# Two gather products of a four-layer graph network: finished chunk by chunk beside the products

## The reference

```python
h = jnp.maximum(_layernorm(x), 0.0)
# layer 3: GCN convolution with self loops, then mish
norm = dinv[row] * dinv[col]                 # dinv = rsqrt(degree + 1)
out = segment_sum((h @ W)[row] * norm[:, None], col) + b
x = x + mish(out)
h = jnp.maximum(_layernorm(x), 0.0)
# layer 4: mean over the neighbours
agg = segment_sum(h[src], dst) / maximum(deg, 1.0)[:, None]
x = x + relu(h @ W_self.T + b_self + agg @ W_neigh.T + b_neigh)
```

## Time and profile before

| | us |
|---|---|
| median of three runs | 3570.17 |
| lowest and highest | 3569.80, 3575.74 |
| the profiled execution | 3569.01 |
| its span | 3566.90 |
| PE busy | 2545.4 (71%) |
| DVE busy | 2710.3 (76%) |
| ACT busy, POOL busy | 1606.4 (45%), 1998.4 (56%) |

### The profile page before, as it was taken

How to read it: one execution, slowest core, us unless ns; L and a number is a source line. 1 busy time by engine, 2 the same in 40 slices (tenths; PEclk the granted TensorE clock), 3 DMA queues, 4 the chain that set the end, 5 groups by cost and what they waited for, 6 DMA issues and landing times. The chain is left out here.

```text
span 3566.9 us, 88132 instructions
## 1 busy us (share of the span) xinstructions
PE 2545.4 (71%) x20080; PEld 1940.4 (54%) x20081; DVE 2710.3 (76%) x8289; ACT 1606.4 (45%) x4084; POOL 1998.4 (56%) x2354
## 2 busy tenths in 40 slices
PE   2433555555555539999999999999992377779399
PEld 1222344343343428888888888888872122334245
DVE  8754777777777739999999999999977799810601
ACT  2011222222222227878787878787866433210201
POOL 1006777777777768888888888888860000000100
PEclk9976767777677669999999999999995699979697
DMA  9992222222222228888888888888866688566182
GB/s 382 414 413 75 81 77 81 77 77 82 77 77 82 72 76 225 228 228 228 224 229 228 229 224 227 230 229 226 227 223 267 249 297 299 212 242 219 75 331 72
DMA packets 699413, 696.66 MB, mean 195 GB/s; under 512 B 48174, under 2 KB 630528, under 8 KB 689632
## 3 DMA queue, kind: packets, MB, share of 16 engines
q1 hardware_dynamic: 478018, 536.77, 44.4%
q10 hardware_dynamic: 195550, 104.71, 12.1%
q0 software_dynamic: 25792, 54.52, 4.5%
HBM read 340.91 MB, written 354.90 MB: 195 GB/s over the span
## 5 line engine op out<-in xcount | busy, mean ns | idle before, releaser
L909 POOL DMA_INDIRECT sorted_rows<-rows,posi x806 | 782.2, 970 | 339.0 <-issue 317.1
L1191 DVE SCALAR_TENSOR_TENSOR acc<-acc,keep,pm 128x256 f32<-128x256 f32 x1504 | 718.3, 478 | 28.5 <-issue 13.1
L1018 POOL TENSOR_SCALAR ohs_e<-iota,rt 128x128 f32<-128x128 f32 x1128 | 661.4, 600 | 12.6 <-DMA rt<-sorted_rows 12.6
L1118 PE MATMUL pm<-ohw_e,ohs_e 128*128 128x128 f32 x3008 | 663.0, 302 | 0.0
L857 PE MATMUL s_peq<-sb_w1bb,eT 128*128 128x256 f32 x806 | 353.1, 532 | 394.9 <-ACT eT L712 376.0
L1027 POOL TENSOR_TENSOR hid<-pre_e,excess 128x512 f32<-128x512 f32 x376 | 517.3, 1376 | 144.5 <-ACT excess L1054 144.5
L1124 PE MATMUL px<-PN,dT 128*128 x4512 | 499.1, 220 | 0.2 <-ACT dT L1061 0.2
L1070 ACT ACTIVATE ohw_e<-ohd_e,rt 128x128 f32<-128x128 bf16 x1504 | 474.7, 386 | 0.0
L1118 PEld LDWEIGHTS pm<-ohw_e,ohs_e 128*128 128x128 f32 x3008 | 459.6, 193 | 0.0
L1135 PE MATMUL ps<-hid,ohs_e 128*128 128x129 f32 x3008 | 417.9, 281 | 1.5 <-POOL hid L1027 1.5
L857 PEld LDWEIGHTS s_peq<-sb_w1bb,eT 128*128 128x128 f32 x806 | 173.1, 265 | 437.2 <-ACT eT L712 428.9
(11 more groups left out here) (300 smaller groups left out, 4438.1 us busy)
## 6 DMA issues: line engine op xcount, KB each, us to landing
count_matrices<-acc SPq DMA_DIRECT2D x1504, 128.0 KB, 2.5
ab<-count_matrices SPq DMA_DIRECT2D x75, 1600.0 KB, 8.7
sorted_rows<-zrow SPq DMA_DIRECT2D x188, 528.0 KB, 10.4
rt<-sorted_rows ACTq DMA_DIRECT2D x184, 528.0 KB, 4.5
arb<-count_matrices SPq DMA_DIRECT2D x25, 1664.0 KB, 6.7
arb<-count_matrices SPq DMA_DIRECT2D x25, 1536.0 KB, 6.4
ef<-in_edge_attr_dram SPq DMA_DIRECT2D x58, 364.0 KB
sorted_rows<-rows,posi POOLq DMA_INDIRECT x806
```

Source lines behind the costliest of these rows:

```text
L909: pool.indirect_dma_start(sortd, bass.IndirectOffsetOnAxis(ap=posi[:, h, c:c + 1], axis=0), rows[:, h, c, :], None).then_inc(s_sc[h], 16)
L1018: last = nc.gpsimd.tensor_scalar(ohs[:, k % BUFS, j, :], iota128[:], rt[:, k, j, D + 1:D + 2], None, ALU.is_equal)
L1118: last = nc.tensor.matmul(pm[:, q, j % 2, P:2 * P], ohs[:, kp % BUFS, j, :], ohw[:, kp % BUFS, j, :], start=True, stop=True)
L1191: nc.vector.scalar_tensor_tensor(acc[:, k % SUMS, j, :], before, keep[:, at:at + 1] if isinstance(at, int) else keep[:, ds(at, 1)], pm[:, ...
```

## The change

Both gathers now run over seven chunks of destinations (six of 512, one of 128) instead of over source tiles. For each chunk PE adds the products of all 25 source tiles into one of two PSUM banks, then goes on with the next chunk, and the sums of the chunk before are finished meanwhile. A load is now a piece: five source tiles by 512 destinations, 2048 consecutive bytes at a time (512 in the last chunk), five slots as before. The first five pieces are issued in `layernorm(1)`, those of the second gather during the first. The features are multiplied with the weight before the gather (`weigh`, 25 products), and all 25 stationary tiles are kept. The sums come out turned, so PE transposes them back (`turn_sums`). In the first gather the mish, the next layernorm and its transposes run per chunk in the same block; POOL has no part in it any more. In the second one the self products (`self_terms`) stand between the products, and the output leaves per chunk at the end. The degree block goes into an earlier stage.

Of the removed lines only the heads are shown; they stand in full above.

```diff
-def evacuate(tag, num, AGT):
...
+            nc.vector.tensor_scalar(dinv[:, 2, :], DEG[:], 1.0, None, ALU.add).then_inc(s_rd, 1)
...
-R = 5
...
-def gather_product(tag, turn, scale, AGT):
...
-    gather_product("2", 0, dinv[:, 0, :], AGT)
...
-    layernorm(2)
-    gather_product("3", 1, None, AGT)
...
+SG = 5
+SLOTS = 5
+NC = len(CUTS)
+NSG = NT // SG
+PIECE = [(c, g) for c in range(NC) for g in range(NSG)] * 2
+ab = gsb("gab", [P, SLOTS, SG, BANK])
+hw = gsb("ghw", [P, NT, D])
+self_ = gsb("g_own", [P, NT, D])
+AG = gsb("g_sums", [P, 2, BANK])
+def tiles(c):
+    return range(4 * c, min(4 * c + 4, NT))
+def load_piece(sp, m):
+    c, g = PIECE[m]
+    a, b = CUTS[c]
+    sp.dma_start(ab[:, m % SLOTS, :, 0:b - a],
+                 arv[0, g * SG:(g + 1) * SG, :, a // P:b // P, :].rearrange("s p q c -> p s (q c)")).then_inc(s_gld[m % SLOTS], 16)
+def gather_chunk(pe, num, turn, c, between):
+    a, b = CUTS[c]
+    n = turn * NC + c
+    if c >= 2:
+        pe.wait_ge(s_ga, n - 1)
+    for s in range(NT):
+        m = n * NSG + s // SG
+        if s % SG == 0:
+            pe.wait_ge(s_gld[m % SLOTS], 16 * (m // SLOTS + 1))
+        if c == 0 and s % 4 == 0:
+            pe.wait_ge(s_gw, turn * NC + s // 4 + 1)
+        last = nc.tensor.matmul(num[:, c % 2, 0:b - a], hw[:, s, :], ab[:, m % SLOTS, s % SG, 0:b - a],
+                                start=(s == 0), stop=(s == NT - 1))
+        if s % SG == SG - 1:
+            last.then_inc(s_gpc, 1)
+        if s in between:
+            between[s]()
+def turn_sums(pe, tn, turn, c):
+    n = turn * NC + c
+    pe.wait_ge(s_ga, n + 1)
+    if c >= 2:
+        pe.wait_ge(s_gy, n - 1)
+    for t in tiles(c):
+        o = t % 4 * P
+        last = nc.tensor.transpose(tn[:, c % 2, o:o + P], AG[:, c % 2, o:o + P], ident[:])
+    last.then_inc(s_gt, 1)
+def copy_sums(act, num, turn, c):
+    a, b = CUTS[c]
+    n = turn * NC + c
+    act.wait_ge(s_gpc, (n + 1) * NSG)
+    if c >= 2:
+        act.wait_ge(s_gt, n - 1)
+    nc.scalar.activation(AG[:, c % 2, 0:b - a], num[:, c % 2, 0:b - a], ACT.Copy).then_inc(s_ga, 1)
+def weigh(pe, zp, turn, c, w):
+    n = turn * NC + c
+    if c >= 2:
+        pe.wait_ge(s_gw, n - 1)
+    for t in tiles(c):
+        o = t % 4 * P
+        last = nc.tensor.matmul(zp[:, c % 2, o:o + P], HT[:, t * P:(t + 1) * P], wl[w][:], start=True, stop=True)
+    last.then_inc(s_gz, 1)
+def first_loads(sp):
+    for m in range(SLOTS):
+        load_piece(sp, m)
+layernorm(1, first_loads)
...
+        def nodes(c):
+            pe.wait_ge(s_nh, c + 1)
+            if c >= 2:
+                pe.wait_ge(s_nc, c - 1)
+            for t in tiles(c):
+                o = t % 4 * P
+                last = nc.tensor.transpose(hp[:, c % 2, o:o + P], H[:, t, :], ident[:])
+            last.then_inc(s_nt, 1)
+        for c in range(NC):
+            weigh(pe, zp, 0, c, "W2")
+        for c in range(NC):
+            between = {}
+            if c >= 1:
+                between[4] = lambda c=c: turn_sums(pe, tn, 0, c - 1)
+            if c >= 2:
+                between[14] = lambda c=c: nodes(c - 2)
+            gather_chunk(pe, num, 0, c, between)
+        turn_sums(pe, tn, 0, NC - 1)
+        nodes(NC - 2)
+        nodes(NC - 1)
...
+        for c in range(NC):
+            stationary(c)
+        for c in range(NC):
+            copy_sums(act, num, 0, c)
+            exp(c)
+            nodes(c)
...
+        def mish(c):
+            k = len(tiles(c))
+            w = k * P
+            t0 = 4 * c
+            z, q, v = Z[:, c % 2, 0:w], Q[:, c % 2, 0:w], V[:, c % 2, 0:w]
+            dve.wait_ge(s_gt, c + 1)
+            for t in tiles(c):
+                o = t % 4 * P
+                last = nc.vector.scalar_tensor_tensor(Z[:, c % 2, o:o + P], tn[:, c % 2, o:o + P], dinv[:, 0, t:t + 1],
+                                                      self_[:, t, :], ALU.mult, ALU.add)
+            last.then_inc(s_gy, 1)
+            dve.wait_ge(s_gy, c + 1)
+            nc.vector.tensor_scalar(q, z, 20.0, None, ALU.min).then_inc(s_zm, 1)
+            dve.wait_ge(s_e, c + 1)
+            link(nc.vector.scalar_tensor_tensor(q, q, 2.0, q, ALU.add, ALU.mult))
+            link(nc.vector.tensor_scalar(v, q, 2.0, None, ALU.add))
+            nc.vector.reciprocal(v, v)
+            link(nc.vector.tensor_tensor(z, z, q, ALU.mult))
+            link(nc.vector.tensor_tensor(z, z, v, ALU.mult))
+            xs = X[:, t0:t0 + k, :].rearrange("p t d -> p (t d)")
+            nc.vector.tensor_tensor(xs, xs, z, ALU.add).then_inc(s_gx, 1)
+            dve.wait_ge(s_gx, c + 1)
+            for u in tiles(c):
+                last = nc.vector.bn_stats(stats[:, u, :], X[:, u, :])
+            link(last)
+            for u in tiles(c):
+                last = nc.vector.bn_aggr(mv[:, u, :], stats[:, u, :])
+            last.then_inc(s_mv, 1)
+            dve.wait_ge(s_sq, c + 1)
+            link(nc.vector.reciprocal(rstd[:, t0:t0 + k], rstd[:, t0:t0 + k]))
+            nc.vector.scalar_tensor_tensor(nbias[:, t0:t0 + k], mv[:, t0:t0 + k, 0], -1.0, rstd[:, t0:t0 + k],
+                                           ALU.mult, ALU.mult).then_inc(s_nb, 1)
...
+        for c in range(NC):
+            mish(c)
+            if c >= 1:
+                nodes(c - 1)
+        nodes(NC - 1)
...
+        for m in range(NC * NSG + SLOTS, 2 * NC * NSG):
+            sp.wait_ge(s_gpc, m - SLOTS + 1)
+            load_piece(sp, m)
+        for c in range(NC):
+            sp.wait_ge(s_gx, NC + c + 1)
+            a, b = CUTS[c]
+            if c < NC - 1:
+                sp.dma_start(out[a:b, :].rearrange("(t p) d -> p t d", p=P), X[:, a // P:b // P, :]).then_inc(s_out, 16)
+            else:
+                sp.dma_start(out[a:N, :], X[0:NR, NT - 1, :]).then_inc(s_out, 16)
...
+        def self_terms(c):
+            if c >= 2:
+                pe.wait_ge(s_sc, c - 1)
+            for t in tiles(c):
+                o = t % 4 * P
+                nc.tensor.matmul(sf[:, c % 2, o:o + P], HT[:, t * P:(t + 1) * P], wl["WsT"][:], start=True, stop=False)
+                last = nc.tensor.matmul(sf[:, c % 2, o:o + P], ones[0:1, :], brow["bs"][:], start=False, stop=True)
+            last.then_inc(s_sf, 1)
+        for c in range(NC):
+            weigh(pe, zp, 1, c, "WnT")
+        for c in range(NC):
+            between = {}
+            if c >= 1:
+                between[4] = lambda c=c: turn_sums(pe, tn, 1, c - 1)
+            if c < NC - 1:
+                between[12] = lambda c=c: self_terms(c)
+            if c == NC - 2:
+                between[20] = lambda c=c: self_terms(NC - 1)
+            gather_chunk(pe, num, 1, c, between)
+        turn_sums(pe, tn, 1, NC - 1)
...
+        def value(c):
+            k = len(tiles(c))
+            dve.wait_ge(s_gt, NC + c + 1)
+            dve.wait_ge(s_sc, c + 1)
+            if c >= 2:
+                dve.wait_ge(s_gx, NC + c - 1)
+            for t in tiles(c):
+                o = t % 4 * P
+                last = nc.vector.scalar_tensor_tensor(Z[:, c % 2, o:o + P], tn[:, c % 2, o:o + P], rdeg[:, t:t + 1],
+                                                      self_[:, t, :], ALU.mult, ALU.add)
+            last.then_inc(s_gy, 1)
+            dve.wait_ge(s_gy, NC + c + 1)
+            xs = X[:, 4 * c:4 * c + k, :].rearrange("p t d -> p (t d)")
+            nc.vector.scalar_tensor_tensor(xs, Z[:, c % 2, 0:k * P], 0.0, xs, ALU.max, ALU.add).then_inc(s_gx, 1)
```

More of the change, by code:

```diff
@@ L104, in build @@
         DEG = tsb("DEG", [P, NT])
+        dinv = tsb("dinv", [P, 3, NT])
+        rdeg = tsb("rdeg", [P, NT])
+        bbc = tsb("bbc", [P, D])
         S = tsb("S", [P, NT + 1, D + 1])
@@ L110, in build @@
         brow = {}
-        for name in ("b1", "b2", "c2", "bs", "bn", "bb2"):
+        for name in ("b1", "bs", "bn"):
             brow[name] = tsb("row_" + name, [1, D])
@@ L130, in build, with layernorm @@
         NQ = -(-NT // 4)
-        def layernorm(r):
+        def layernorm(r, ahead=None):
             with ExitStack() as ctx:
@@ L136, in layernorm, with _ @@
                 block = ctx.enter_context(nc.Block())
+                if ahead:
+                    @block.sync
+                    def _(sp):
+                        ahead(sp)
                 @block.vector
@@ L173, in _ @@
                             last.then_inc(s_ln["turned"], 1)
-        def evacuate(tag, num, AGT):
-            with nc.Block() as block:
-                @block.vector
-                def _(dve):
-                    for c, (a, b) in enumerate(CUTS[0::2]):
-                        nc.vector.tensor_copy(AGT[:, a:b], num[:, 2 * c, 0:b - a])
-                @block.scalar
-                def _(act):
-                    for c, (a, b) in enumerate(CUTS[1::2]):
-                        nc.scalar.activation(AGT[:, a:b], num[:, 2 * c + 1, 0:b - a], ACT.Copy)
         with ExitStack() as srt:
@@ L297, in _ @@
                         act.dma_start(to if to.shape[0] == ED else to[:], fr).then_inc(s_ld, 16)
```

(35 more changed lines are left out.)

315 lines of the change are left out of this document (109 added, 206 removed).

## The result

The changed kernel takes 3480.02 us, the median of four runs (3478.00 to 3483.75), where the kernel before takes 3571.33 on the same chip (four runs, 3569.80 to 3575.74): ratio 0.9744, 95% interval 0.9727 to 0.976, 91 us less. Forecast were 3494, 76 less. The profiled execution took 3479.23, its span 3477.4; against the 3569.0 of before that is 89.8.

What follows compares the result with a forecast made beforehand. PE bounds the gathers; most of 98.6 us where it stands nearly still should be hidden. First gather 171.2 plus second 172.4 make 343.6 against 419.4 us, 75.8 less: 3494 us, range 3476 to 3526.

Steps and rivals of the forecast that it cites:

- weigh: Before each gather's chunks: 25 products with the weight at the low clock, 0.43 us each, 10.8 us.
- the cold start: Start of the long products in each gather, before the clock is high: 2.2 us on top of 129.0.
- the transposes: Groups of four inserted in both gathers: 0.78 us a group, 7.0 us in the first gather, 3.9 in the second.
- the end of the first gather: Chunk 6 and the unhidden chain behind mish(5), through normalization and the one-tile chain to the barrier: 22.2 us.
- the pairs: Second gather: 25 self products, each with a one-row product, 0.64 us a pair, 16.0 us; bounds 11.0 and 32.0.
- The main step: Behind layernorm(1): most of the 98.6 us with PE nearly still leaves the path; PE stays the bound; 75.8 us less.
- The lower case of the range: Transposes in both gathers at half the price, if the high clock halves it: 6 us less.
- I take half: Second gather: a pair's 1.28 us at the low clock taken as 0.64 at the high clock.
- Rival 1: Clock falls at inserted work: 4.8 us at each of six self-product groups, 29 us, 3523; chance 0.14.
- the forecast's 3550: Rival's further case: clock also falls at the first gather's nine transpose groups, 27 us more; chance 0.03 within 0.14.
- Do the loads keep up?: Both gathers: 2048-byte runs need 284 and 264 GB/s; 415 taken, no cost; at 228, 47 us more.
- Nothing there: Block of degrees moved to an earlier stage, beside a transfer already waited for: costs nothing in its new place.

Runs made afterwards that it cites:

- first_only: Changed kernel with the second gather and final block as in the kernel before, degrees computed ahead: 3505.2 us, ratio 0.9813 to the kernel before.
- after2: The changed kernel run once more, unaltered, as base of the last group of runs: 3485.18 us, ratio 0.9753 to the kernel before.
- act_order: Changed kernel with ACT copying chunk 6's first-gather sums ahead of chunk 5's root and normalization: 3771.29 us on the 3856.34 us chip, ratio 0.9776.
- up: Kernel before with only the changed kernel's edits ahead of the gathers: 3565.2 us against 3570.38, ratio 0.9981.
- spread: Changed kernel with a chunk's four pairs apart, behind products 7, 10, 13 and 16: 3762.57 us on the 3856.34 us chip, ratio 0.9753.
- bias_dve: Changed kernel without the 25 one-row products, DVE adding the last layer's bias: 3748.51 us on the 3856.34 us chip, ratio 0.9722.
- bias2: Changed kernel without the 25 one-row products, DVE adding the bias, run in the last group: 3463.84 us, ratio 0.9692 to the kernel before.

## Why the prediction was right, and where its terms were off

The mechanism held, and the time lies in the range (3476 to 3526), 4 us above its low end. That the sum of the tail came within 5.4 us is in part luck: weigh (4.5), the cold start (4.4), the transposes (4.8) and the end of the first gather (1.0) were 14.7 us too dear, the pairs (4.8) and the falls of the clock (5.1) 9.9 us too cheap.

- *The main step*, that most of what stood alone (98.6 us) goes beside the products and PE stays the bound, is shown: 60.3 us by the first gather alone, 21 to 23 by the second, tail 420.1 to 338.8 and 337.1. The forecast's shares were 59.3 and 16.5, with the wait of 6.7 us in front of the second gather in the first share; first_only still pays that wait. Drawn as in the forecast, the stretches of the changed kernel give 230.5 - 162.9 = 67.6 and 188.9 - 175.3 = 13.6.
- *First gather, weigh* (10.8) was too dear, twice: 9.0 and 8.1. I took the low clock for all of it, but the clock rises within it. The stretches from 3140, 3142 and 3144 us:

```profile
3140.00:3142.00 2.00, 2.00 (x12) 2.00 (x10) 0.00 (x0) 0.40 (x2) 0.00 (x0) 0.50 0.04 8
3142.00:3144.00 2.00, 2.00 (x14) 1.88 (x13) 1.14 (x4) 1.53 (x7) 0.00 (x0) 0.76 0.00 0
3144.00:3146.00 2.00, 1.66 (x13) 1.52 (x13) 1.50 (x6) 1.79 (x8) 0.00 (x0) 1.00 0.00 0
```

  In after2 it rises later, 6.0 us after weigh's first product instead of 3.5, and there the first long product starts 9.4 us after weigh's first and not 8.7.
- *The cold start* (2.2 in each gather) is paid in weigh, and the long products begin at 1.00. I had charged weigh the low clock to its end and the long products the start as well: 4.4 us too much.
- *Transposes*: 0.44 a group and not 0.78, as 0.196 each had been read at the low clock: 14 groups, 4.8 us. The lower case of the range.
- *Self products*: 0.83 a pair and not 0.64, 4.8 us more than forecast. The term was mis-sized by the step "I take half": the high clock doesn't halve the price of a pair in which a one-row product follows a full one.
- *Rival 1* came true in part and at a third of its price. The clock did fall at groups of self products, but at 9 of 24, and at 1.7 us each and not 4.8, since the fall comes behind the group and not in it (a group followed by slow products takes 3.22 us from start to start like any other), and the long products were back at the high clock within 4 us. That makes 5 us in the profiled execution, 3 in after2. At transposes it never fell: chunks 0 to 5 of the first gather have clock 1.00 with nine groups in them, so the forecast's 3550 is out. The Trainium skill (TensorE: Matmul & The Clock Gate, Part 4: PE-mode transpose) says that transposes don't count as PE work; this trace gives no sign of it for four of them between long products.
- *The end of the first gather* (22.2): 21.2. Mish(5) takes 10.9 as said. Behind it the path goes over ACT (normalization, copy, table load, exponential, see act_order) and then over DVE for the one tile. The forecast let the table loads run while ACT idles; this one, 1.28 us, has no idle time to hide in.
- *Do the loads keep up?* They do, 387 GB/s against 284. The value taken, 415 from packets of 3.7 KB, was somewhat high. What the Trainium skill says (DMA: Bandwidth & Descriptors, "Why small descriptors are slow"), 3 cycles over the bytes' own, would give by estimate 407 from these 415 (64/67 over 116/119); the run measured 387, so the rule gives a part of the fall.
- *Nothing there* for the degrees was right in their new place: from the first transpose of that stage to the first product of the next one there are 21.5 us before, 21.8 and 21.5 in the two profiles of the changed kernel. What their old block cost in front of the gather no run shows by itself; before, it lasts 3.2 us (3147.58 to the issue of the loads at 3150.82), and PE's wait behind it is 10.80 us, against 7.18 in first_only's second gather, which has no such block. But the edits ahead of layernorm(1) gave some 5 us (ratio 0.9981) which no term of mine had; they were costed at nothing. That is as much as the sum missed in the tail, and its mechanism stays open: the gain is there before the degree operations run (up), which leaves the loads of three rows and the places of the buffers, not told apart. The profile's 8.3 us there are these 5 and scatter from one execution to the next.

Of the 14 us between 3494 and 3480.0, 5.4 are the terms of the tail and 5.2 the edits ahead (3570.38 - 3565.2); they make 3483.4, and 3.4 us are left, about the scatter of the runs.

## What to carry to other kernels

Where two engines take turns between barriers, cut the work so that one engine finishes a piece while the other runs the next piece's products; the price is what PE is asked to do in addition, and it was small here (0.44 us for four transposes). Before pricing a small product at the high clock, look at what stands next to it: the pair with a one-row product cost nearly four times a plain product, and the bias cost nothing on the engine that copies the result anyway (0.69 us for four tiles on DVE with it and without). Before moving a small operation to the front, look at what stands behind it on its engine: the early copy left the exponential where it was. Count a cold start once, at the first products after the pause.

## What the hardware showed that was not expected

- One-row products alternating with full ones start 0.41 to 0.42 us apart at the high clock, full ones among themselves 0.22. A pair costs 0.82 to 0.83 us whether it stands in a group or alone.
- Groups of four such pairs (3.3 us) let the granted clock fall behind them in 9 of 24 cases and not at fixed ones; pairs standing alone never did (24 of them, in spread), four plain products never did (24 groups). Whether it is the one-row products, or that four pairs of them stand together, only spread's one execution tells apart.
- While the 25 weigh products ran, the granted clock rose from 0.50 to 1.00, 3.5 and 4.5 us after their start in the two gathers of the first profile, 6.0 and 2.8 us in after2.
- On ACT the exponential follows the normalization 1.31 us later when only a table load (1.28 us) stands between them.
- One chip ran the kernel before in 3856 us where the other groups of runs had 3570 to 3574, with almost all of the difference ahead of layernorm(1); the saving was of like size there (bias_dve -107.8 us, bias2 -109.7).
